# The mixture-of-experts stage of a two-layer decoder: rows weighed before the gather, scatters that add into one row per token, and loop and last part in one block

## The reference

```
xn = layernorm(x) * gamma + beta                    # 2048 tokens, width 256
probs = clip(softmax(clip(xn @ router_w.T)), 1e-8, 1)   # 8 experts
topk_p, topk_i = top_k(probs, 2)
for eid in range(8):
    xe = xn * dense_gate[:, eid]                    # 0 where the expert isn't chosen
    gate, up = split(xe @ gate_up_w[eid].T)         # 512 each
    out += (silu(gate) * up) @ down_w[eid].T
return layernorm((x + out) + x)
```

## Time and profile before

| | |
|---|---|
| median of 3 runs | 1420.37 us |
| the profiled execution: its own time | 1422.48 us |
| the profiled execution: its span | 1420.8 us |
| PE busy | 1197.0 us (84%) |
| DVE busy | 881.0 us (62%) |
| ACT busy | 743.3 us (52%) |
| POOL busy | 608.3 us (43%) |
| front block of the experts | about 1075 to 1145.7 us of the span |
| loop block | 1145.7 to 1388.2 us |
| last block | 1388.2 to the end |

### The profile page before, as it was taken

The page is one execution under the profiler, slowest core; times in us unless marked ns, Lnnn a source line. Parts: engine busy times, 40 slices in busy tenths (PEclk is TensorE's granted clock), DMA queues, the critical chain, the costliest instruction groups (busy, mean ns, idle before and its releaser), DMA issues. The chain is left out here.

```text
span 1420.8 us, 25057 instructions
## 1 busy us (share of the span) xinstructions
PE 1197.0 (84%) x8059; PEld 873.5 (61%) x8060; DVE 881.0 (62%) x1545; ACT 743.3 (52%) x2046; POOL 608.3 (43%) x664
## 2 busy tenths in 40 slices
PE   7888589575999999999899999998984368999970
PEld 4544367454667767776666777665763357777750
DVE  2588799773445555563445566665886656677745
ACT  2598457334556556655555566652661035555532
POOL 1155457557436223322633322101664336666635
PEclk9999799797899999999999999999996569999995
DMA  9100000010010010001010001005401001111105
GB/s 303 27 1 0 0 1 2 1 30 16 16 30 16 16 30 16 16 1 31 15 25 17 5 16 45 1 1 224 133 1 45 23 19 49 44 48 48 48 33 178
DMA packets 36136, 56.04 MB, mean 39 GB/s; under 512 B 6528, under 2 KB 27392, under 8 KB 36032
## 3 DMA queue, kind: packets, MB, share of 16 engines
q1 hardware_dynamic: 32288, 44.47, 10.5%
q0 software_dynamic: 3744, 10.23, 2.2%
HBM read 34.90 MB, written 9.31 MB: 31 GB/s over the span
## 5 line engine op out<-in xcount | busy, mean ns | idle before, releaser
L2016 DVE TENSOR_REDUCE ga_neg_top<-ps 128x1 f32<-128x128 f32 (+7 forms) x256 | 181.9, 752 | 195.2 <-PE ps L1786 194.8
L1897 ACT ACTIVATE ga_e<-ps,ga_neg_top 128x128 f32<-128x128 f32 (+7 forms) x256 | 188.2, 743 | 7.5 <-DVE ga_neg_top L2016 6.8
L1906 ACT COPY ga_e_tr<-ps 128x512 f32<-128x512 f32 (+3 forms) x192 | 92.0, 479 | 174.6 <-PE ps L1795 172.1
L1795 PE MATMUL ps<-ident,ga_e 128*128 128x128 f32 x1152 | 165.1, 279 | 0.8 <-DVE ga_e_tr L2024 0.8
L1811 PE MATMUL ps<-ga_e_tr,ga_v 128*64 128x256 f32 x1152 | 151.7, 391 | 4.1 <-ACT ga_att L1914 4.1
L1795 PEld LDWEIGHTS ps<-ident,ga_e 128*128 128x128 f32 x1152 | 123.3, 142 | 28.0 <-ACT ga_e L1897 14.7
L2024 DVE COPY ga_e_tr<-ps 128x128 f32<-128x128 f32 (+3 forms) x192 | 105.8, 551 | 35.1 <-PE ps L1795 34.8
L2528 DVE TENSOR_TENSOR ex_w_lo<-ex_gate_up,ex_w_hi 128x1024 fp32r<-128x1024 f32 x78 | 92.7, 1229 | 42.1 <-ACT ex_w_hi L2493 42.0
L1971 POOL TENSOR_TENSOR ga_q_lo<-shared,ga_q_hi 128x1024 fp32r<-128x1024 f32 x15 | 35.5, 2370 | 175.5 <-ACT ga_q_hi L1887 175.5
L2493 ACT CAST ex_w_hi<-ex_gate_up 128x1024 fp32r x78 | 77.9, 1046 | 50.5 <-PEq L2189 35.0
L1811 PEld LDWEIGHTS ps<-ga_e_tr,ga_v 128*64 128x64 f32 x1152 | 72.4, 136 | 48.9 <-issue 23.3
(11 more groups left out here) (330 smaller groups left out, 2738.7 us busy)
## 6 DMA issues: line engine op xcount, KB each, us to landing
shared<-shared SPq DMA_DIRECT2D x80, 128.0 KB, 2.4
ex_gate_up<-in_ex_gate_up SPq DMA_DIRECT2D x1, 8192.0 KB, 24.3
ex_down<-in_ex_down SPq DMA_DIRECT2D x1, 4096.0 KB, 35.7
x_tr<-in_x_tr SPq DMA_DIRECT2D x4, 512.0 KB, 7.3
x_nat<-in_x SPq DMA_DIRECT2D x1, 2048.0 KB, 11.7
xn_rows<-x_tr SPq DMA_DIRECT2D x8, 256.0 KB, 2.1
x_tr<-choice_rows SPq DMA_DIRECT2D x8, 256.0 KB, 4.9
shared<-choice_rows SPq DMA_DIRECT2D x8, 256.0 KB, 5.5
```

The source lines that it names most:

```text
L1795: last = nc.tensor.transpose(ps_tr[n % 2][:, (kb - k0) * P:(kb - k0 + 1) * P], e[half][t % 2][:, kb * P:(kb + 1) * P], core.ident[:])
L1897: nc.scalar.activation(e[half][t % 2][:, 0:blocks(t) * P], ps_scores(t, half), ACT.Exp, bias=neg_top[t % 2][:, half:half + 1], accum_out=s ...
L1906: nc.scalar.copy(e_tr[g % 2][:, k0:k1, half, t % 2 * P:(t % 2 + 1) * P], ps_tr[n % 2][:, 0:(k1 - k0) * P].rearrange("p (k t) -> p k t", t= ...
L2016: nc.vector.tensor_reduce(neg_top[t % 2][:, half:half + 1], ps_scores(t, half), AX.X, ALU.max, negate=True).then_inc(top_ready, 1)
```

## The change

- Front block. The gates no longer go through the inversion. As soon as each gate is known, ACT multiplies all normalised rows by it (32 activations of 128x256), and SP writes them to `gated_rows`, one row per pair (16 DMAs of 256 KB in place of 8). At the block's start ACT doubles x (4 activations of 128x1024) and SP writes it to `summed_rows` (4 DMAs of 512 KB and one of 128 KB for the unused rows). The one-hots and values become bf16, with two column groups in place of three; the running sum over the experts is done in 3 steps; the experts of the tiles (`past` and on) are computed behind the one-hots. POOL has three more small memsets and no more part in the values. POOL issues the gather of tile 0 at the end of this block, after all 16 writes have landed.
- Loop. The gather brings rows of `gated_rows` straight into `row`; the multiply and the buffer `tokens_in` go. PE waits for the gather itself. The scatter adds to `summed_rows`, one row per token, and waits for the scatter before.
- Last part. It is in the loop's block. SP waits for the last scatter and loads 8 DMAs of 256 KB in place of 16. POOL's and DVE's adds go. POOL, ACT and DVE reach their parts behind their loops.

The core of the diff:

```diff
@@ front block, SP
-                    sp.dma_start(xn_rows.rearrange("(n p) d -> p n d", p=P)[:, tiles, :], xn[:, tiles, :]).then_inc(xn_written, 16)
+                for n in range(TILES // DOUBLED):
...
+                    sp.dma_start(summed_rows[0:N, :].rearrange("(n p) d -> p n d", p=P)[:, tiles, :],
+                                 doubled[n // len(HALVES)][:, HALVES[n % len(HALVES)], :]).then_inc(summed_written, 16)
+                sp.dma_start(summed_rows[N:N + P, :], doubled[0][:, 0, :]).then_inc(summed_written, 16)
+                for i in range(2):
+                    for g in range(GROUPS_OF_TILES):
...
+                        sp.dma_start(gated_rows[i * N:(i + 1) * N, :].rearrange("(n p) d -> p n d", p=P)[:, tiles, :],
+                                     gated[i][:, tiles, :]).then_inc(gated_written, 16)
@@ front block, POOL
-                        nc.gpsimd.tensor_tensor(tile_values[:, i, :, part, :], in_tile[:, i], of_tiles(value), ALU.mult).then_inc(values_ready, 1)
+                pool.wait_ge(gated_written, 16 * 2 * GROUPS_OF_TILES)
+                pool.wait_ge(sources_ready, 1)
+                fetch(pool, 0)
@@ front block, ACT
+                for n in range(TILES // DOUBLED):
...
+                    nc.scalar.activation(doubled[...], core.x_nat[:, tiles, :], ACT.Copy, scale=2.0).then_inc(doubled_ready, 1)
...
+                for i in range(2):
+                    act.wait_ge(gates_ready, i + 1)
+                    for t in range(TILES):
+                        last = nc.scalar.activation(gated[i][:, t, :], xn[:, t, :], ACT.Copy, scale=gates[:, i, t:t + 1])
@@ front block, PE (at_place and choice_values are bf16)
-                        last = nc.tensor.matmul(ps_slots, at_place[:, t, :], tile_values[:, i, t, :, :],
+                        last = nc.tensor.matmul(ps_choice, at_place[:, n, :], choice_values[:, n, :, :], start=(n == 0), stop=(n == 2 * TILES - 1))
@@ front block, DVE
-                for x in range(1, EXPERTS):
-                    link(nc.vector.tensor_tensor(ends[:, x:x + 1], ends[:, x - 1:x], count[:, x:x + 1], ALU.add))
+                for n, distance in enumerate((1, 2, 4)):
+                    link(nc.vector.tensor_tensor(summed, reach[n][:, LEFT:], reach[n][:, LEFT - distance:LEFT - distance + EXPERTS], ALU.add))
...
+                one_hot(in_tile[:], ...).then_inc(in_tile_ready, 1)
...
+                nc.vector.tensor_tensor(choice_values[:, :, 0, :], in_tile[:], of_tiles(tile_iota[:]), ALU.mult)
+                nc.vector.tensor_scalar(choice_values[:, :, 1, :], in_tile[:], place[:, 0:1], None, ALU.mult).then_inc(choice_values_ready, 1)
+                for i in range(2):
+                    one_hot(at_place[:, i * TILES:(i + 1) * TILES, :], place_f[:, i, :], place_iota, P).then_inc(places_ready, 1)
@@ loop, POOL
+        def fetch(pool, g):
+            nc.gpsimd.tensor_copy(tile_source[:], column(source, g)).then_inc(source_ready, 1)
+            pool.wait_ge(source_ready, g + 1)
+            nc.gpsimd.indirect_dma_start(row, None, gated_rows,
+                                         bass.IndirectOffsetOnAxis(ap=tile_source[:], axis=0)).then_inc(gathered, 16)
...
                 def step(g, t, u1, u2, u3):
-                    if t is not None:
-                        pool.wait_ge(gathered, 16 * (t + 1))
-                        need(pool, rows_tr_ready, t)
-                        nc.gpsimd.tensor_tensor(row, tokens_in, column(slot_gate, t).to_broadcast([P, D]), ALU.mult).then_inc(row_ready, 1)
-                    if g is not None:
-                        need(pool, row_ready, g)
+                    if g is not None and not at(g, 0):
+                        need(pool, rows_tr_ready, g)
+                        fetch(pool, g)
                     if u3 is not None:
                         pool.wait_ge(down_copied, u3 + 1)
...
+                        need(pool, scattered, 16 * u3)
-                        nc.gpsimd.indirect_dma_start(choice_rows, ...tile_choice...,
-                                                     rows_out, None).then_inc(scattered, 16)
+                        nc.gpsimd.indirect_dma_start(summed_rows, ...tile_target...,
+                                                     rows_out, None, compute_op=ALU.add).then_inc(scattered, 16)
@@ loop, PE
-                        pe.wait_ge(row_ready, t + 1)
+                        pe.wait_ge(gathered, 16 * (t + 1))
@@ last part, now behind the loops of the same block
-                    nc.gpsimd.tensor_tensor(scratch[:, tiles, :], scratch[:, tiles, :], xn[:, tiles, :], ALU.add).then_inc(sum_ready, 1)
-                    link(nc.vector.scalar_tensor_tensor(core.x_nat[:, tiles, :], core.x_nat[:, tiles, :], 2.0, scratch[:, tiles, :],
-                                                        ALU.mult, ALU.add))
+                sp.wait_ge(scattered, 16 * SLOT_TILES)
...
-                    for i in range(2):
-                        sp.dma_start(parts[i][:, tiles, :], rows[:, tiles, :]).then_inc(choices_loaded[g], 16)
+                    sp.dma_start(xn[:, tiles, :], rows[:, tiles, :]).then_inc(sums_loaded[g], 16)
```

More of the change, by code:

```diff
@@ L2104, in stage_experts @@
     BATCHED = BANK // D
+    LEFT = EXPERTS // 2
+    CHOICE_PARTS = 2
+    DOUBLED = 4
+    HALVES = [slice(n, n + DOUBLED) for n in range(0, TILES // 2, DOUBLED)]
     GROUPS_OF_TILES = TILES // GROUP
@@ L2120, in stage_experts @@
         ones = core.sb(ctx, "ex_ones", [P, P], BF16)
[L2121 removed]
         count_int = core.sb(ctx, "ex_count_int", [P, EXPERTS], I32)
         ends = core.sb(ctx, "ex_ends", [P, EXPERTS])
+        reach = [core.sb(ctx, f"ex_reach{i}", [P, LEFT + EXPERTS]) for i in range(3)]
         starts = core.sb(ctx, "ex_starts", [P, EXPERTS])
@@ new lines, in _ @@
+                link(nc.vector.tensor_tensor(starts[:], ends[:], count, ALU.subtract))
+                link(nc.vector.scalar_tensor_tensor(work[:], starts[:].unsqueeze(1).to_broadcast(by_tile), float(P), ps_rank[:, 0:TILES, :],
+                                                    ALU.mult, ALU.add))
+                link(nc.vector.tensor_tensor(picks[:], picks[:], work[:].unsqueeze(1).to_broadcast([P, 2, TILES, EXPERTS]), ALU.mult))
+                link(nc.vector.reduce_sum(slots_f[:], picks[:], AX.X))
@@ L2354, in _ @@
                 link(nc.vector.tensor_copy(expert[:], expert_f[:]))
-                link(nc.vector.tensor_scalar_mul(starts[:], starts[:], float(P)))
-                link(nc.vector.tensor_tensor(work[:], ps_rank[:, 0:TILES, :], starts[:].unsqueeze(1).to_broadcast(by_tile), ALU.add))
-                for i in range(2):
-                    link(nc.vector.tensor_tensor(picks[i][:], picks[i][:], work[:], ALU.mult))
-                    link(nc.vector.reduce_sum(slots_f[:, i, :], picks[i][:], AX.X))
@@ L2371, in _ @@
-                link(nc.vector.tensor_copy(gate_parts[:, 0].bitcast(F32R), gates[:]))
-                link(nc.vector.tensor_tensor(gate_parts[:, 1], gates[:], gate_parts[:, 0], ALU.subtract))
-                for i in range(2):
-                    last = one_hot(in_tile[:, i], tile_f[:, i, :], slot_iota, SLOT_COLUMNS)
-                last.then_inc(in_tile_ready, 1)
-                link(nc.vector.tensor_scalar(slots_part[:], slots[:], P - 1, None, ALU.bitwise_and))
-                link(nc.vector.tensor_copy(place_f[:], slots_part[:]))
@@ L2393, in _ @@
+                in_tiles, in_place = (ps_choice[:, i * SLOT_COLUMNS:(i + 1) * SLOT_COLUMNS] for i in range(CHOICE_PARTS))
+                link(nc.vector.tensor_scalar(unused[:], in_tiles, 0.0, place[:, 0:1], ALU.is_equal, ALU.mult))
+                link(nc.vector.scalar_tensor_tensor(unused[:], in_tiles, float(P), unused[:], ALU.mult, ALU.add))
+                link(nc.vector.scalar_tensor_tensor(choice_f[:], in_place, float(2 * N), unused[:], ALU.add, ALU.add))
                 link(nc.vector.tensor_copy(choice[:], choice_f[:]))
-                link(nc.vector.tensor_scalar(token[:], choice[:], N - 1, None, ALU.bitwise_and))
+                nc.vector.tensor_scalar(source[:], choice[:], 2 * N - 1, None, ALU.bitwise_and).then_inc(sources_ready, 1)
@@ L2510, in _ @@
                 lagged(act, SLOT_TILES, 2, step, turns=True)
+                for g in range(GROUPS_OF_TILES):
+                    act.wait_ge(offset_ready, g + 1)
+                    for t in range(g * GROUP, (g + 1) * GROUP):
+                        last = nc.scalar.activation(xn[:, t, :], xn[:, t, :], ACT.Identity, bias=offset[:, t:t + 1],
+                                                    scale=rstd[:, t:t + 1])
+                    last.then_inc(final_ready, 1)
             @block.vector
```

190 lines of the change are left out of this document (84 added, 106 removed).

## The result

The changed kernel takes 1501.05 us, the median of 4 runs from 1499.11 to 1502.67, beside 1420.38 us for the kernel before on the same chip: a ratio of 1.056, 95% interval 1.053 to 1.059. The forecast was 1500 us, range 1448 to 1550. The profiled execution took 1501.37 us, with a span of 1499.6.

What follows compares the result with a forecast made beforehand. The prediction took POOL, the engine without a gap, to bound the loop at 5.48 us a turn. Loop +96, front -2.5 and last part -13.6 gave +80 on the median of 1420.37: 1500 us, range 1448 to 1550.

Steps and rivals of the forecast that it cites:

- The ring: Loop: gather waits for PE's transposes, scatter queues behind it, ACT, DVE, PE wait in turn; 14.61 us per two turns, +64 us.
- The clock: Loop: PE idles in each pair of turns, its granted clock falls, 1.3 us lost per pair: +23 us, ends 0 and +30.
- The add: Loop: the adding scatter also reads the row it adds to, landing 0.5 us later: +9 us, upper end +26.
- the favourable case: Loop: the scatter's issue takes 0.98 us instead of 1.51: -0.27 us a turn, -9 us.
- the upper end of 26: Loop: an adding scatter costs a second landing of 1.46 us: +26 us.
- The routing: Front block, from ranks to tokens: fewer small steps, bf16 products, no waits between halves; -10 us, down to -12.
- The switch: From `source` to PE's first gate matmul: POOL's copy, gather, 6.44 us drain, then barrier and weights, 14.8 us: +7.5 us.
- the "short drain" end of the prediction: End of the front block: POOL's drain takes 0.30 us instead of 6.44, making this stretch +1.4 us.
- The last part: Last scatter's landing to kernel end: eight groups at POOL's 1.56 us each, drain of 6.44, 25.8 us in all: -13.6 us.
- The faster rival: Loop: POOL's relief decides, ACT never waits, turns run at PE's pace of about 5.1 us: 1391 us, chance 0.09.

Runs made afterwards that it cites:

- the run with 8 fillers: The changed kernel with 8 further identity matmuls, results unused, at each of two places where PE idles in a pair of turns: 1490.5 us.
- the scatter first: The changed kernel with the scatter of four steps back ahead of the gather in each step of POOL's loop: 1394.3 us.
- the version with the indices ahead: The changed kernel with scatter ahead of gather, two buffers of output rows, and both index columns copied a step ahead: 1381.8 us.

## Why the prediction was right in the sum and off in its terms

**The ring** (+64 forecast) was right in place, in links and nearly in length. The ring alone costs 74 us in the kernel before. Summed in the changed kernel, from 1305.98 (start of PE's turn) to 1323.33, it is 17.35 us:

| link | forecast | measured |
|---|---|---|
| PE's turn to its rows transposed | 3.66 | 5.22 |
| semaphore to POOL | 0.05 | 0.25 |
| copy, pause, gather | 1.99 | 1.98 |
| copy, pause, scatter | 2.53 | 2.68 |
| landing | 1.46 | 2.30 |
| ACT's copy to PE's turn | 4.92 | 4.92 |

The two links that grew most are the ones that the prediction had priced apart, clock and add. The semaphore and the issue of the scatter grew by 0.20 and 0.15 us, 6 us in 17.5 pairs; the "shortest gaps" that the 0.05 was read from aren't this semaphore's.

**The clock** (+23 forecast) was 1.56 us a pair in the round shown, 1.3 forecast: 17.5 x 1.56 = 27. That PE falls to 1.2 GHz behind its idle and that the loss lies in the ring is shown by the windows above and by the section that is back at 3.65 us with fillers. How much of the kernel's time it is isn't shown as cleanly: the run with 8 fillers got 11 us, and gave some back in the copy beside DVE and ahead of the loop's steady part (its first scatter is issued at 1162.72 instead of 1160.10).

**The add** (+9 forecast) is the term that was mis-sized in the loop. The landing grew by 0.84 us, the prediction's value was 0.5. And the issue was counted as today's 1.51 us with a lower end of 0.98, as if an add cost POOL nothing: each of the 39 adding scatters takes 1.56 to 1.63 us here, the writing ones of the run without the add 1.00 in the median (0.98 to 1.88), so that the favourable case was gone. Together with the lower clock that goes with it, the add is worth 30 us in this order, above the upper end of 26. The Trainium skill (Collectives: The Full Stack, The bandwidth ceiling: the fold count and why AG ≠ RS ≠ AR) says of ReduceScatter that its adding DMAs have half the rate because they read two sources. The trace doesn't come out at a half. One adding scatter of the changed kernel and one writing scatter of the run without the add, both by the DMA view over 1315.5 to 1318.5 us (packets, MB, share of 16 engines):

```profile
q0 software_dynamic: 144, 0.13, 38.4%
...
q0 software_dynamic: 48, 0.13, 12.2%
```

For the same bytes the add has three times the packets and three times the engines' time. The landing rose by only 0.84 us on 1.46, less than by that rule.

**The routing** (-10, down to -12): `source` is ready at 1131.21 (1131.03 + 0.18) where `token` was at 1145.13, -13.9, of which 1.25 stand already at the step behind the ranks (1116.92 against 1118.17); that part may be chance, since `source` is ready anywhere from 1130.7 to 1135.3 us in the versions of the changed kernel. The other 12.7 are the forecast's lower end and a little more; the bf16 products of a half take 1.25 us, where 3.67 had been kept as the upper bound.

**The switch** (+7.5) is the term that failed at the front. From `source` to the first gate matmul are 9.5 us against 7.3, +2.2. The drain was taken at 6.44, from its only row, and added behind the gather; it was 3.38 us and began 0.3 us before the gather's issue did, so it reached 1.9 us beyond it. The run without an indirect DMA in that block (34 ns) shows that the drain is long because of the gather; the "short drain" end of the prediction, +1.4, was the nearer one.

**The last part** (-13.6): -16.9. The drain at the end came as forecast, 6.60 us. Off is POOL's pace: 1.21 us a group (1489.24 to 1490.45) in place of 1.56, since its root takes 0.69 us, not 1.11. Eight groups by 0.35 are 2.8 of the 3.3 us. Why the root was slower before wasn't tried, but the rows of the kernel before point at DVE's add of the rows (L2575), which the change removes: the root of 1.11 us at 1412.62 starts under it, and the last root, with no such add beside it, takes 0.69:

```profile
1412.47 0.69 DVE L2575 SCALAR_TENSOR_TENSOR x_nat<-x_nat,shared 128x512 f32<-128x512 f32 x1
...
1414.59 0.69 POOL L2554 TENSOR_TENSOR ex_rstd<-ex_var_eps,neg_half 128x2 f32<-128x2 f32 x1 [0.59 <-DVE ex_var_eps L2584]
```

**The faster rival** was priced at 1391 us, "it decides only if the scatter isn't queued behind the gather". With the scatter first the kernel took 1394.3. The same working that gave the loss gave the repair, but the closeness of the two times is luck. The rival's 29 us were 13 in the loop, from a turn at PE's own pace of 5.1 us. With the scatter first the turn is 5.53 us and the stretch from the first gate matmul to the last scatter's issue only 2.7 us shorter than before (224.8 against 227.5): POOL stays full, since its copy for the gather takes 0.91 us beside DVE. The two ends gave 26 us in place of 16.

## What to carry to other kernels

Ask of every in-order queue what stands behind a wait that was moved earlier: taking 0.94 us of work per turn from the one engine without a gap cost 74 us here, because that work was also the slack between its reader and its writer, and an unrelated DMA was queued behind it. When no engine is full and three of them wait in turn, add up one round of the ring; the cheapest repair is an order (the scatter that frees others first) or one more buffer, and either gave 107 to 108 us. And a part that moves a block's border should be priced with the drain at both places, the old and the new.

## What the runs showed of the hardware that I had not expected

- POOL's drain isn't a wait for transfers alone. A drain's row can begin before POOL's last instruction ends, so what counts is how far it reaches beyond that. At the end of the changed kernel it reaches 6.4 us beyond, although the last scatter had landed 13 us before (1477.85 against 1491.2); in the kernel before 6.44 (1381.6, behind the landing), in the run with the last part in its own block 6.3. Behind a block with one gather it is 1.9 us. Without an indirect DMA in the block next to nothing: the front block's drain in the kernel before is 8.1 us long (L2189, 1126.9 to 1135.0) but ends with POOL's last multiply at 1134.99, and the last block's 0.30 us end 0.05 behind POOL's last instruction. All the long ones, in every run, have 77 or 78 indirect DMAs in their block. Whether their number sets it wasn't tried.
- An indirect scatter that adds costs POOL 0.6 us more to issue than one that writes (1.59 against 1.00 in the same place of the ring), beside the later landing. Beside DVE's subtraction the writing one takes longer too, 1.51 us in the earlier trace rows, and up to 1.9.
- The pause of about 0.8 us ahead of an indirect DMA stays when nothing has to be copied just before it: 0.87 us from the end of PE's transposes to the gather in the version with the indices ahead.
- Edits of POOL's queue alone moved PE's granted clock in the loop: 0.84 in the changed kernel, 0.94 without the add, 1.00 with the scatter first.
